# A fused conditional FFN layer: gate and up by tiles of two samples, from gathered rows of weight products

## The chip, the cores and the metric

One core of a Trainium2 chip runs the kernel. Five engines matter: TensorE (PE, matmuls and transposes, with PEld for its weight loads), VectorE (DVE), ScalarE (ACT), GpSimd (POOL) and SyncE (SP, which here only issues DMAs). Each takes its instructions in program order and waits on semaphores. The metric is the device time of one execution in microseconds; a comparison gives the median over rounds on the same chip.

## The reference

There are 32 samples of 64 rows by 1024 numbers, so 2048 rows. Two layers follow one another:

```
x = x + ffn0(cond0(x))    # cond0: a 64x64 matrix per sample; ffn0: W, bias and 8 LoRA terms
x = x + ffn1(cond1(x))    # below
Bx    = einsum('bni,bri->bnr', x,  B[adapter_ids])     # rank 16, own adapter of each sample
cond1 = einsum('bnr,bor->bno', Bx, A[adapter_ids])     # 1024 wide
gate  = cond1 @ Wg.T ;  up = cond1 @ Wu.T              # 2752 hidden units, 4-bit codes
ffn1  = (silu(gate) * up) @ Wd.T                       # codes with a scale per 64
```

The hidden units are 21 chunks of 128 and a tail of 64. Since `cond1` has rank 16 per sample, gate is `Bx @ (A' Wg')`: the kernel multiplies each chunk of the gate and up weights with all 8 adapters' A first, which gives a 128 x 128 product (8 adapters x 16 ranks by 128 hidden units). That is the "weight product" below.

## The kernel before, in words

Single-precision numbers are split into a high and a low part of a rounded 32-bit type (`F32R`), and a product is three matmuls: high x high, high x low, low x high.

**Two phases.** The first phase goes over 16 tiles of 128 rows (two samples each) and computes `x1`, the first layer's output, and from it `Bx` of the second (`adapter_bx`, with a bias). The second phase goes over 96 slots: 6 groups of 3 or 4 chunks (`GROUPS`) times 16 row tiles. A slot is one tile's down matmuls over the group's chunks (`down`), the store of the sum by an accumulating DMA (`accumulate`), and, between them, other work. Slots 80 to 95, the last group, add the result read back from memory instead.

**Decoding.** A unit is the gate part `("g", c)`, the up part `("u", c)` or the down part `("d", c)` of a chunk's weights (`("t", c)`: gate and up of the tail). ScalarE computes the 8 linear functions of the codes (`line`), VectorE folds them by minimum and maximum (`decode`, `combo`) and scales the result. The number of VectorE's steps per slot is planned by `RATE` (`STEPS_B`), and so is the slot in which a unit is turned (`TURN_AT`, `turn_unit`). A turned gate or up unit is multiplied with A by `adapter_ga` in the slot behind it (16 records for 8 full-precision matmuls), near the slot's end. ScalarE copies the product out of PSUM (`evac_ga`, into `ga_f`), and GpSimd splits it (`split_ga`, into `st_hi` and `st_lo`). Units 0 to 11 of gate and up are decoded in the first phase, units 12 to 21 in slots 12 to 72.

**Gate and up.** Before the change `Bx` of a tile is masked by VectorE (`mask_bx`): of the 128 rows (8 adapters x 16) only those of the sample's own adapter are kept, and GpSimd splits it (`split_bx`) into `bx_hi` and `bx_lo`. `gate_up(g, b, k)` makes chunk k of group g for a block b of 512 columns (4 tiles), three matmuls of 512 columns for the gate and three for the up part:

```
for m, ps in enumerate((ps_g, ps_u)):
    for p, (w, v) in enumerate(((st_hi, bx_hi), (st_hi, bx_lo), (st_lo, bx_hi))):
        ins = pe.matmul(ps, w[:, c % ST, m, :], v[:, cols], start=p == 0, stop=p == 2)
```

`gate_ups_at` puts the passes of the next block one by one into the slots of this one. ScalarE takes the SiLU (`silu`), VectorE multiplies (`product`), ScalarE makes the high part (`inter_hi`) and VectorE the low (`inter_lo`) that `down` reads.

**Order.** Every engine's order is written out by hand, slot by slot. GpSimd's in a slot is `split_ga` of the unit turned in the slot before, if there is one, and then `accumulate` of the slot before. In TensorE's slot `gate_up` stands behind the down matmuls of all chunks but the last two, and `adapter_ga` behind all but the last.

## Time and profile before

| what | value |
|---|---|
| median of 3 runs | 1005.73 us (1005.17 to 1006.11) |
| span of the profiled execution, first to last instruction | 1007.3 us |
| TensorE busy | 992.0 us, 98% |
| VectorE busy | 892.6 us, 89% |
| ScalarE busy | 773.8 us, 77% |
| GpSimd busy | 286.6 us, 28% |
| mean granted TensorE clock | 0.994 of full speed |
| DMA | 126.31 MB, mean 125 GB/s |
| share of the chain that ended last | PE 94%, DVE 3%, ACT 1%, DMA 1% |

The profiled execution has no separate time of its own beside its span; the span stands 1.6 us, 0.2%, above the median of the runs. A busy matmul is a record with the length of its whole passage; records overlap, so the cost of one in a stream is the distance between starts. A row of a timeline is start, duration, engine, line and operation (out<-in), the number merged, and in brackets the idle time before it and what ended it.

### The profile page before, as it was taken

What the parts mean: (1) busy time and instruction counts of PE and PEld (TensorE: products, weight loads), DVE (VectorE), ACT (ScalarE), POOL (GpSimd) and SP (SyncE); (2) the same over time, 40 slices, a digit from 0 to 9 for tenths busy, and PEclk for the clock granted to TensorE, in tenths of its full rate; (3) what the DMA queues carried; (4) which work ended last, traced back from release to release, by engine and by line L of the source; (5) the groups of instructions that cost most, each with busy time, mean ns of one, the idle gap of its engine ahead of it and who ended that gap; (6) DMA issues with size and microseconds to landing.
All of it is one profiled execution on the core that took longest, in us unless ns stands there. A gap on an engine that the chain in (4) does not pass through costs nothing.

```text
span 1007.3 us, 15039 instructions
## 1 busy us (share of the span) xinstructions
PE 992.0 (98%) x5314; PEld 849.9 (84%) x5314; DVE 892.6 (89%) x1308; ACT 773.8 (77%) x929; POOL 286.6 (28%) x269
## 2 busy tenths in 40 slices
PE   6999999999999999999999999999999999999998
PEld 5898899889898878888888888888888888888887
DVE  3999999989999979999999999999999999962353
ACT  4788888878878869988888889889888888853220
POOL 4015533633542421132312241113304123321000
PEclk8999999999999999999999999999999999999999
DMA  9846446347334337767475456656465563664766
GB/s 246 220 139 157 101 109 174 87 99 197 86 89 103 71 57 126 144 113 139 68 138 98 95 106 125 108 103 126 89 122 106 104 122 69 124 139 74 195 220 230
DMA packets 73658, 126.31 MB, mean 125 GB/s; under 512 B 7504, under 2 KB 49504, under 8 KB 73584
## 3 DMA queue, kind: packets, MB, share of 16 engines
q0 software_dynamic: 15200, 51.41, 31.8%
q1 hardware_dynamic: 57056, 72.89, 24.4%
q10 hardware_dynamic: 1328, 1.05, 0.3%
q8 instruction: 43, 0.70, 0.3%
q14 instruction: 31, 0.25, 0.1%
HBM read 66.61 MB, written 67.11 MB: 133 GB/s over the span
## 4 chain that ended last, share of the span: by engine, by line
PE 94%; DVE 3%; ACT 1%; DMA 1%; issue 1%; ACTq 0%; DVEq 0%
PE ps_z L1173 23%; PE ps_y L1173 23%; PE ps_z L1017 16%; PE ps_gu L1148 12%; PE ps_gu L1075 4%; PE ps_t L1063 4%; PE ps_t L1075 3%; PE ps_y L1004 3%; PE ps_gu L1035 2%; PE ps_t L1027 1%; DMA la<-in_L_ffn_lora_A 1%; DVE val L789 1%; ACT ring L610 1%; PE ps_z L994 1%; DVE val L791 0%
## 5 line engine op out<-in xcount | busy, mean ns | idle before, releaser
L610 ACT ACTIVATE ring<-codes 128x1024 f32<-128x1024 int32 x455 | 455.3, 1053 | 2.4 <-DVE val L789 1.1
L789 DVE TENSOR_TENSOR val<-val,ring 128x512 f32<-128x512 f32 x520 | 327.8, 689 | 2.5 <-ACT ring L610 2.1
L791 DVE SCALAR_TENSOR_TENSOR val<-ring,val 128x512 f32<-128x512 f32 x390 | 247.8, 690 | 6.0 <-ACT ring L610 5.5
L524 POOL TENSOR_TENSOR st_hi<-ga_f,one 128x128 fp32r<-128x128 f32 x42 | 78.4, 1866 | 227.0 <-ACT ga_f L650 226.9
L582 POOL DMA_DIRECT2D out<-staged x80 | 69.3, 926 | 235.2 <-ACT staged L736 226.3
L722 ACT ACTIVATE inter<-ps_gu 128x512 f32<-128x512 f32 x88 | 52.6, 598 | 92.4 <-PE ps_gu L1148 91.9
L1017 PE MATMUL ps_z<-we_hi,y_hi 128*128 128x512 f32 x256 | 104.7, 409 | 0.2 <-DVE y_lo L850 0.2
L931 DVE TENSOR_TENSOR inter<-ps_gu,inter 128x512 f32<-128x512 f32 x88 | 60.2, 684 | 47.1 <-ACT inter L722 46.2
L1017 PE MATMUL ps_z<-we_hi,y_lo 128*128 128x512 f32 x256 | 100.3, 392 | 0.0
L1017 PE MATMUL ps_z<-we_lo,y_hi 128*128 128x512 f32 x256 | 100.0, 391 | 0.0
L547 POOL TENSOR_TENSOR bx_hi<-bx_f,one 128x128 fp32r<-128x128 f32 x16 | 43.8, 2740 | 142.5 <-DVE bx_f L862 142.5
L1173 PE MATMUL ps_z<-wd_late_hi,in_hi 128*128 128x512 f32 x256 | 81.1, 396 | 0.0
L1173 PE MATMUL ps_y<-wd_late_hi,in_hi 128*128 128x512 f32 x256 | 80.3, 395 | 0.3 <-DVE wd_late_lo L844 0.3
L937 DVE TENSOR_TENSOR in_lo<-inter,in_hi 128x512 fp32r<-128x512 f32 x88 | 61.7, 701 | 17.1 <-ACT in_hi L728 17.0
L1173 PE MATMUL ps_z<-wd_late_lo,in_hi 128*128 128x512 f32 x240 | 74.3, 390 | 0.0
L1173 PE MATMUL ps_z<-wd_late_hi,in_lo 128*128 128x512 f32 x240 | 74.3, 389 | 0.0
L1173 PE MATMUL ps_y<-wd_late_lo,in_hi 128*128 128x512 f32 x240 | 74.0, 390 | 0.0
L1173 PE MATMUL ps_y<-wd_late_hi,in_lo 128*128 128x512 f32 x240 | 74.0, 389 | 0.0
L1148 PE MATMUL ps_gu<-bx_hi,st_hi 128*128 128x512 f32 x176 | 69.3, 394 | 0.7 <-DVE inter L931 0.7
L606 ACT ACTIVATE val<-codes 128x1024 f32<-128x1024 int32 x65 | 68.4, 1053 | 1.8 <-DMA codes<-in_L_ffn_gate_codes 1.8
L1148 PE MATMUL ps_gu<-bx_hi,st_lo 128*128 128x512 f32 x176 | 69.0, 392 | 0.0
L1148 PE MATMUL ps_gu<-bx_lo,st_hi 128*128 128x512 f32 x176 | 69.0, 392 | 0.0
(141 smaller groups left out, 1888.5 us busy)
## 6 DMA issues: line engine op xcount, KB each, us to landing
out<-staged POOLq DMA_DIRECT2D x80, 512.0 KB, 5.6
codes<-in_L_ffn_down_codes SPq DMA_DIRECT2D x21, 512.0 KB, 4.0
xs<-in_x SPq DMA_DIRECT2D x16, 512.0 KB, 4.0
out<-in_L_ffn_bias SPq DMA_DIRECT2D x4, 2048.0 KB, 14.5
out<-xs POOLq DMA_DIRECT2D x16, 512.0 KB, 5.5
ring<-out SPq DMA_DIRECT2D x16, 512.0 KB, 4.3
out<-ring SPq DMA_DIRECT2D x15, 512.0 KB, 2.9
codes<-in_L_ffn_gate_codes SPq DMA_DIRECT2D x12, 512.0 KB, 5.2
```

Of the source, the lines that this page charges most:

```text
L524: pool.tensor_tensor(hi, src, one[:, :].to_broadcast([P, P]), ALU.mult).then_inc(ga_step, 1)
L582: pool.dma_start(out_rows[t * P:(t + 1) * P, :], staged[:, place, :], accum_op=ALU.add).then_inc(acc_out[place], 16)
L606: act.activation(val_of(n), codes[:, n % 2, :], ACT.Relu, bias=offset, scale=slope).then_inc(lines, 1)
L610: act.activation(ring[:, (k - 1) % RING, :], codes[:, n % 2, :], ACT.Identity, bias=offset, scale=slope).then_inc(lines, 1)
L789: ins = dve.tensor_tensor(into, into, line, pick)
L791: ins = dve.scalar_tensor_tensor(out=into, in0=line, scalar=add, in1=into, op0=ALU.add, op1=pick)
L931: dve.tensor_tensor(inter[:, q % 2, :], ps_u[:, :], inter[:, q % 2, :], ALU.mult).then_inc(inter_ready, 1)
L937: dve.tensor_tensor(in_lo[:, b % 2, k, :], inter[:, q % 2, :], in_hi[:, b % 2, k, :].bitcast(F32), ALU.subtract).then_inc(in_lo_ready, 1)
L1017: ins = pe.matmul(ps_z[:, half], y[:, jc, :], w[:, jc, half], start=jc == 0 and p == 0, stop=jc == DC - 1 and p == 2)
L1075: ins = pe.matmul(ga_bank(n), ad_at[:, q, :, :].rearrange("p n r -> p (n r)"), wt[:, m % 2, q, :], start=q == 0, stop=q == DC - 1)
L1148: ins = pe.matmul(ps, w[:, c % ST, m, :], v[:, cols], start=p == 0, stop=p == 2)
L1173: ins = pe.matmul(ps_o[slot % 2][:, h * HALF:(h + 1) * HALF], v[:, b % 2, k, s * P:(s + 1) * P], wd_of(c, w)[:, h * HALF:(h + 1) * HALF], ...
```

## The change

Gate and up are computed per tile of 128 columns (two samples) instead of per block of 512. Instead of three matmuls over 128 masked rows there is one over 96 rows: 2 samples x 16 ranks, three times, the high part twice and the low part once.

- The split products no longer stay on chip. `st_hi` and `st_lo` are 3 places deep (12 before), and SyncE stores each into a table in memory per group (`store_table`).
- For each of the 96 works (group, tile) GpSimd gathers the 96 rows of the two samples' own adapters (high, low, high) by an indirect DMA (`fetch`, into `gath`, 3 places). The row numbers come from `selections` on VectorE, at the kernel's start.
- `bx_p` holds the matching `Bx`: ScalarE adds the bias (`bias_bx`), TensorE puts the own rows of each sample into three places of 32 rows (`place_bx`, three full-precision matmuls), ScalarE writes the high part (`place_hi`) and VectorE the low (`low_bx`). `mask_bx` and `split_bx` are gone.
- `gate_up(w)` is one matmul per chunk for gate and one for up, 6 or 8 per work. It runs two slots ahead (`AHEAD`).
- SiLU, product and the split of `inter` are per work, with widths of 384 or 512.
- Two lines of `BY_GROUP` change, so that gate and up units of groups 4 and 5 are turned some slots earlier than down units.

```diff
-    ST = 12
+    ST = 3
+    INR = 3
+    GS = 3
+    AHEAD = 2
+    FETCH = 4
+    KP = 96
...
-        [("d", 15), ("g", 17), ("u", 17), ("d", 16), ("g", 18), ("u", 18), ("d", 17), ("d", 18)],
-        [("g", 19), ("d", 19), ("u", 19), ("g", 20), ("u", 20), ("d", 20), ("t", TAIL), ("d", TAIL)],
+        [("g", 17), ("u", 17), ("d", 15), ("g", 18), ("u", 18), ("d", 16), ("d", 17), ("d", 18)],
+        [("g", 19), ("u", 19), ("g", 20), ("u", 20), ("t", TAIL), ("d", 19), ("d", 20), ("d", TAIL)],
...
+            def store_table(n):
...
+                sp.wait_ge(ga_split, m + 1)
+                for part, st in enumerate((st_hi, st_lo)):
+                    sp.dma_start(tables[g][part * P:(part + 1) * P, cols],
+                                 st[:, m % ST, :, :].rearrange("p a i -> p (a i)")[:, 0:width].bitcast(F32)
+                                 ).then_inc(table_in[m % ST], 16)
...
+            def fetch(w):
+                g, t, _ = work_of(w)
+                if t == 0:
+                    for k in range(ST):
+                        pool.wait_ge(table_in[k], 16 * 2 * len(range(k, LAST_GU[g] + 1, ST)))
+                if w == 0:
+                    pool.wait_ge(select_step, 8)
+                wait(pool, u_mm, w - GS + 1)
+                width = len(GROUPS[g]) * 2 * P
+                pool.indirect_dma_start(gath[0:KP, w % GS, 0:width].bitcast(F32), None, tables[g][:, :],
+                                        bass.IndirectOffsetOnAxis(ap=row_at[0:KP, t:t + 1], axis=0)
+                                        ).then_inc(gath_in[w % GS], 16)
...
             store_x1(NT - 1)
-            split_bx(NT - 1)
+            for w in range(GS):
+                fetch(w)
...
-            for slot in range(LAST + 1):
+            for slot in range(WORKS):
                 if is_gu(TURN_AT.get(slot - 1)):
                     split_ga(TURN_AT[slot - 1])
-                if slot > 0:
+                if GS <= slot + FETCH - 1 < WORKS:
+                    fetch(slot + FETCH - 1)
+                if 0 < slot <= LAST:
                     accumulate(slot - 1)
...
+            def place_bx(t):
+                pe.wait_ge(select_step, 4)
+                pe.wait_ge(bx_biased, t + 1)
+                wait(pe, bx_split, t)
+                own = place_of[:, PER * t:PER * (t + 1), :].rearrange("p s r -> p (s r)")
+                for part in range(KP // SQ):
+                    ins = pe.matmul(place_bank(t)[part * SQ:(part + 1) * SQ, :], own, bx_f[:, :], start=True, stop=True)
+                ins.then_inc(bx_placed, 1)
...
-            def gate_up(g, b, k):
+            def gate_up(w):
+                g, t, _ = work_of(w)
+                pe.wait_ge(gath_in[w % GS], 16 * (w // GS + 1))
                 if g == 0:
+                    pe.wait_ge(bx_split, t + 1)
+                for m, (ps, free, done) in enumerate(((ps_g, silu_ready, g_mm), (ps_u, inter_ready, u_mm))):
+                    wait(pe, free, w)
+                    for k in range(len(GROUPS[g])):
+                        ins = pe.matmul(ps[:, k * P:(k + 1) * P], gath[0:KP, w % GS, (2 * k + m) * P:(2 * k + m + 1) * P],
+                                        bx_p[0:KP, t * P:(t + 1) * P], start=True, stop=True)
+                    ins.then_inc(done, 1)
```

The order on GpSimd in the second phase, before the change: each pair of splits is followed by accumulates (`out<-staged`), one per slot.

```order
L582 DMA out<-staged 128x1024 x12
L524 TENSOR_TENSOR st_hi<-ga_f,one 128x128
L526 TENSOR_TENSOR st_lo<-ga_f,st_hi 128x128
L582 DMA out<-staged 128x1024 x3
L524 TENSOR_TENSOR st_hi<-ga_f,one 128x128
L526 TENSOR_TENSOR st_lo<-ga_f,st_hi 128x128
```

And of the change, from slot 15 on (L574 and L576 are the two splits, L603 is the gather, L637 the accumulate):

```order
L637 DMA out<-staged 128x1024
L574 TENSOR_TENSOR st_hi<-ga_f,one 128x128
L576 TENSOR_TENSOR st_lo<-ga_f,st_hi 128x128
L603 DMA gath<-table1,row_at 96x1024
L637 DMA out<-staged 128x1024
L603 DMA gath<-table1,row_at 96x1024
L637 DMA out<-staged 128x1024
```

A gather now stands between each split and the accumulate behind it, and one in every other slot as well.

TensorE's order around a product of a unit with A (L1075, `ps_t<-wt,ad_at`), before the change, to the next slot's gate and up pass.

```order
L1075 MATMUL ps_t<-wt,ad_at 128x128 x8
L1173 MATMUL ps_y<-wd_late_hi,in_hi 128x512 x2
L1173 MATMUL ps_y<-wd_late_lo,in_hi 128x512 x2
L1173 MATMUL ps_y<-wd_late_hi,in_lo 128x512 x2
L1173 MATMUL ps_z<-wd_late_hi,in_hi 128x512 x2
L1173 MATMUL ps_z<-wd_late_lo,in_hi 128x512 x2
L1173 MATMUL ps_z<-wd_late_hi,in_lo 128x512 x2
L1173 MATMUL ps_z<-wd_early_hi,in_hi 128x512 x2
L1173 MATMUL ps_z<-wd_early_lo,in_hi 128x512 x2
L1173 MATMUL ps_z<-wd_early_hi,in_lo 128x512 x2
L1148 MATMUL ps_gu<-bx_hi,st_hi 128x512
```

The same in the change (L1174 the product with A, L1271 down, L1246 gate and up), through to the next slot's gate and up pass:

```order
L1174 MATMUL ps_t<-wt,ad_at 128x128 x8
L1271 MATMUL ps_y<-wd_late_hi,in_hi 128x512 x2
L1271 MATMUL ps_y<-wd_late_lo,in_hi 128x512 x2
L1271 MATMUL ps_y<-wd_late_hi,in_lo 128x512 x2
L1271 MATMUL ps_z<-wd_late_hi,in_hi 128x512 x2
L1271 MATMUL ps_z<-wd_late_lo,in_hi 128x512 x2
L1271 MATMUL ps_z<-wd_late_hi,in_lo 128x512 x2
L1271 MATMUL ps_z<-wd_early_hi,in_hi 128x512 x2
L1271 MATMUL ps_z<-wd_early_lo,in_hi 128x512 x2
L1271 MATMUL ps_z<-wd_early_hi,in_lo 128x512 x2
L1246 MATMUL ps_gu<-bx_p,gath 128x128 x8
```

What stands between the product with A and the next gate and up pass is as it was: one chunk of this slot and two of the next. The pass itself is 8 matmuls of 128 columns where 6 of 512 were.

VectorE's first instructions, before the change and then with it (`lb` and `lbq` are made by the operations on `wt`):

```order
L868 TENSOR_SCALAR lw<-lw 128x8
L870 TENSOR_TENSOR wt<-wt,lw 128x1024
L872 COPY lbq<-wt 128x1024
```

```order
L947 TENSOR_SCALAR odd_i<-part_i 128x1
L950 TENSOR_SCALAR ids_rank<-ad_ids 128x32
L952 CAST odd_f<-odd_i 128x1
L954 TENSOR_TENSOR place_of<-ids_rank,less_rank 128x512
L957 SCALAR_TENSOR_TENSOR ids_step<-ids_rank 128x16
L960 TENSOR_SCALAR diag<-odd_f 128x1
L961 COPY diag<-odd_f 128x1
L963 SCALAR_TENSOR_TENSOR ids_own<-ids_step,odd_f,ids_rank 128x16
L966 TENSOR_SCALAR row_at<-ids_own,row_base 96x16
L971 TENSOR_SCALAR lw<-lw 128x8
```

Nine small operations moved ahead of the first one; the second of them needs `ad_ids` from memory.

## Rows read from the trace of the kernel before

**Rows 1.** Busy time by stage; `us, PE busy (x) PEld DVE ACT POOL, PEclk, DMA share, GB/s`

```profile
42.70:350.00 307.30, 307.27 (x1952) 275.14 (x1953) 296.09 (x466) 258.45 (x300) 126.17 (x113) 1.00 0.47 117
...
366.00:893.00 527.00, 526.75 (x2549) 442.89 (x2548) 518.73 (x749) 457.00 (x556) 130.96 (x109) 1.00 0.58 108
...
893.00:1007.30 114.30, 111.02 (x494) 91.70 (x492) 42.86 (x50) 26.01 (x37) 10.52 (x16) 1.00 0.66 184
```

**Rows 2.** Timeline of TensorE, slot 8; start, us, engine, line, operation

```profile
409.30 0.39 PE L1148 MATMUL ps_gu<-bx_hi,st_hi 128*128 128x512 f32 x1
...
410.66 0.61 PE L1173 MATMUL ps_y<-wd_early_hi,in_hi 128*128 128x512 f32 x2
```

**Rows 3.** Timeline of TensorE, full-precision matmuls of 128 weight columns

```profile
201.04 1.95 PE L1075 MATMUL ps_gu<-wt,ad_at 128*128 128x128 f32 x16
...
202.74 0.48 PE L1017 MATMUL ps_z<-we_hi,y_hi 128*128 128x512 f32 x1
...
53.68 1.84 PE L1129 MATMUL ps_gu<-bias_c,ad_bt 128*128 128x1 f32 x16
```

**Rows 4.** Timelines of one turned unit: TensorE, ScalarE, GpSimd, TensorE

```profile
625.02 1.95 PE L1075 MATMUL ps_t<-wt,ad_at 128*128 128x128 f32 x16
...
627.19 0.27 ACT L650 ACTIVATE ga_f<-ps_t 128x128 f32<-128x128 f32 x1
...
627.61 1.83 POOL L524 TENSOR_TENSOR st_hi<-ga_f,one 128x128 fp32r<-128x128 f32 x1 [11.07 <-ACT ga_f L650]
...
629.51 1.32 POOL L526 TENSOR_TENSOR st_lo<-ga_f,st_hi 128x128 fp32r<-128x128 f32 x1
...
630.78 1.75 POOL L582 DMA_DIRECT2D out<-staged  x2
...
630.89 0.39 PE L1148 MATMUL ps_gu<-bx_hi,st_hi 128*128 128x512 f32 x1
```

**Rows 5.** Timelines, GpSimd free and TensorE's next pass: first and last unit

```profile
446.17 1.76 POOL L582 DMA_DIRECT2D out<-staged  x2
...
444.19 0.39 PE L1148 MATMUL ps_gu<-bx_hi,st_hi 128*128 128x512 f32 x1
...
896.73 1.74 POOL L582 DMA_DIRECT2D out<-staged  x2
...
895.98 0.39 PE L1148 MATMUL ps_gu<-bx_hi,st_hi 128*128 128x512 f32 x1
```

**Rows 6.** DMA issues: operation, number, KB each, us to landing

```profile
cond_bd<-in_L_cond_weights POOLq DMA_DIRECT2D x32, 16.0 KB, 2.1
...
ring<-out SPq DMA_DIRECT2D x16, 512.0 KB, 4.3
...
out<-staged POOLq DMA_DIRECT2D x80, 512.0 KB, 5.6
```

**Rows 7.** Timelines of TensorE and GpSimd, hand-over between the phases

```profile
355.85 1.09 PE L1027 MATMUL ps_y<-ident,xs 128*128 128x128 f32 x8 [1.48 <-DVE xs L857]
...
357.66 0.77 PE L1148 MATMUL ps_gu<-bx_hi,st_hi 128*128 128x512 f32 x1 [0.72 <-DVE inter L931]
...
360.36 2.29 PE L1035 MATMUL ps_z<-x1t,ad_bt 128*128 128x128 f32 x16
...
356.42 0.87 POOL L511 DMA_DIRECT2D out<-xs  x1
```

**Rows 8.** Start: GpSimd's timeline, DMA issues, VectorE's timeline

```profile
2.82 0.61 POOL L493 DMA_DIRECT2D ad_ids<-in_itok_B  x1
...
ad_ids<-in_itok_B POOLq DMA_DIRECT2D x1, 16.0 KB, 7.5
...
9.72 0.69 DVE L872 COPY lbq<-wt 128x1024 f32<-128x1024 f32 x1
```

**Rows 9.** Costliest groups and one row of GpSimd's timeline: splits

```profile
L524 POOL TENSOR_TENSOR st_hi<-ga_f,one 128x128 fp32r<-128x128 f32 x42 | 78.4, 1866 | 227.0 <-ACT ga_f L650 226.9
...
203.38 0.40 POOL L524 TENSOR_TENSOR st_hi<-ga_f,one 128x128 fp32r<-128x128 f32 x1 [1.20 <-ACT ga_f L650]
```

323 lines of the change are left out of this document (187 added, 136 removed).

## The prediction, made before the changed kernel ran

> **What bounds the kernel now.** I read the busy time by stage first [rows 1]. The reader is to see two engines full at once: TensorE is busy 307.27 of 307.30 us in the first phase and 526.75 of 527 us in slots 0 to 73, and VectorE is busy 518.73 of the same 527. Only behind 893 us, where decoding is over, has VectorE room (42.86 of 114.30). So a saving on TensorE alone is worth at most 527 - 518.7 = 8.3 us up to slot 73, and its whole size only behind it. ScalarE (457 of 527) and GpSimd (131 of 527) have room by busy time. GpSimd's matters here for its order, not for its load: it stands most of a slot for `ga_f`, then splits it.
>
> **TensorE: what gate and up cost before and after.** A chunk of 512 tokens took 410.66 - 409.30 = 1.36 us for six matmuls, 0.227 us each [rows 2]; 88 of them are 119.7 us. The change puts 64 times 8 and 32 times 6 matmuls of 128 columns there (704). No narrow matmul of the rounded type is in the trace. The nearest rows are full-precision ones, each of which is recorded as two: 16 records take 202.74 - 201.04 = 1.70 us, 0.106 each, and 16 that move one single column take 1.84 us with the tail of the last [rows 3]. Columns moved don't set this; loading 128 weight columns does. The new ones load 128 weight columns each, from 96 rows, so I take 0.11 (the 0.106, and a little for the wide matmul behind). Bounds: a quarter of 0.227, 0.057, below; two records, 0.212, above. With 0.11, 8 cost 0.88 and 6 cost 0.66, in all 77.4 us, 42 less than before. By place: slots 0 to 73 had 71 chunk passes (96.6 us) and get 60 x 0.88 + 14 x 0.66 = 62.0, which is -34.6; slots 74 to 95 had 14 (19.0) and get 4 x 0.88 + 16 x 0.66 = 14.1, which is -5; the rest is in the hand-over between the phases.
>
> The Trainium skill, TensorE: Matmul & The Clock Gate, "Back-to-back issue gap", has a stream of loads and matmuls at 128 columns cost about 81 ns each. The rows have 106 ns, and the rows are used; by the page TensorE would have some 704 x 0.025 = 18 us less to do.
>
> **The new wait, and who stands behind it.** GpSimd's order in a slot s that follows a turned gate or up unit is: split `ga_f` (high, low), then the gather for tile s+3, then the accumulate. TensorE uses tile s+3 in slot s+1, behind the first two of four chunks. In every other slot the gather is issued nearly two slots ahead; in these it is issued only when the split is done. The trace has each step of this already. Adapter product from 625.02; `ga_f` at 627.19; high part at 627.61, low part at 629.51; the next thing GpSimd does starts at 630.78 in the trace; and the gate and up matmul of slot s+1 starts at 630.89 [rows 4]. So there is nothing between GpSimd being free and TensorE's need. There are 19 such units, from the first (GpSimd free 446.17, TensorE there 444.19, 1.98 late) to the last (896.73 against 895.98, 0.75 late) [rows 5]; over all 19 pairs, read in the same way, GpSimd is 0.62 us late in the mean. What comes on top is the gather from issue to landing. Nothing in the trace is a gather; the nearest transfers take 2.1 us for 16 KB, 4.3 for a 512 KB read from memory and 5.6 for a 512 KB accumulate [rows 6]. A gather brings 96 rows of 4 KB, 384 KB, from memory: on the line between 2.1 and 4.3 that is 3.8. Bounds 2.1 and 5.6. So TensorE stands 0.62 + 3.8 = 4.4 us, 19 times: 84 us (52 to 118).
>
> The Trainium skill, DMA: Bandwidth & Descriptors, "Anatomy of one DMA", fits a transfer issued by GpSimd as 2.0 us plus its bytes over 436 GB/s. An estimate by that page is 2.9 us for a gather, and 19 x 3.5 = 67 us of standing instead of 84. That page's line has no descriptor work for rows by index.
>
> Behind the standing matmul on TensorE are the last two chunks of the slot, so nothing can run ahead: the engine takes its instructions in order. VectorE meets the same wait half a slot later, at its product of that tile, and ScalarE at the SiLU. Both are less than a slot ahead, so they stand too and don't get the time back. VectorE's 8.3 us bound no longer matters: 34.6 us of saved matmuls are taken off the 84, and 49.4 stay.
>
> **The clock.** In the hand-over TensorE stood 1.48 and 0.72 us within 3.5 us, and behind it six matmuls took 360.36 - 357.66 = 2.70 us instead of 1.36 (the 1.2 instead of the 2.4 GHz level), and the next sixteen 2.29 instead of 1.95 [rows 7]. That is 1.7 us lost. Some of the 19 stands will do that. The row has it at 2.2 us of standing in all, and other short stands don't show it; I take 8 of 19, 14 us (0 to 32).
>
> **First phase.** `place_bx` adds three full-precision matmuls with 32 weight columns and 128 moved, 15 times here: six records. At 0.106 each that is 0.64 us; at a quarter of 0.227, 0.34 [rows 2, 3]. TensorE is full here, so it all counts: I take 0.5, 7.5 us (5 to 9.6). ScalarE gets the bias and two small scalings per tile, VectorE two small differences for one masking; both have room by [rows 1] (258 and 296 of 307). GpSimd loses `split_bx`, which nothing waited for. The stores of the tables go through SyncE's queue behind loads of codes that it issues early, and are hidden: a table is complete slots before its group's first gather. If that cover failed, the first gather of a group would come a few us late, five times in all.
>
> **Start.** `selections` stands first on VectorE and needs `ad_ids`, issued at 2.82 and landing 7.5 us later, at 10.3, and some 0.5 later still behind four more iotas [rows 8]. Nine small operations (about 2.2 us) and then the scaling of `lb`, which ended with `lbq` at 9.72 + 0.69 = 10.4, bring it to about 15.2. The transposes of it had room for only part of that: I take +2 us (0 to 3).
>
> **Hand-over.** The first gather stands on GpSimd behind the store of the last x1 tile, issued at 356.42 and 0.87 long: it lands at 357.3 + 3.8 = 361.1. The first gate and up matmul waits for it, and so does the transpose of x1 behind it (355.85 before, about 362 now). From there to the first down matmul one gate and up pass less lies in the way, so of 6 us 4 stay (2 to 6) [rows 7].
>
> **Sum.** 1007.3 + 2 + 7.5 + 4 + 84 - 34.6 + 14 - 5 = 1079 us for a profiled span. The span stands 1.6 us above the median of the runs, 1005.73, so 1078.
>
> **Rivals.**
> *A, the forecast.* Its ends: all low, 1007.3 + 7 + 52 - 34.6 - 5 = 1027, all high, 1007.3 + 2 + 9.6 + 6 + 118 + 32 - 34.6 - 5 = 1135; on the scale of the median 1025 to 1134. Chance 0.66.
> *B, the gather's issue is held up as the splits are.* The high part of a split took 1.87 us in the mean and 1.83 in [rows 4], and one of the same size only 0.40 [rows 9]; what differs is what VectorE runs beside it. If writing the gather's descriptors is held up likewise, 1.5 us come on top of each stand, and up to 3: 19 x 2.3 = 44 in the middle, 1122. Against it: two issues of accumulates took 1.75 us in [rows 4], beside the same VectorE work. The Trainium skill, SBUF — State Buffer, has this as a rule (the two engines share a port pair, and descriptors that GpSimd writes wait for it); it would give this rival's time. Chance 0.12.
> *C, a narrow matmul of the rounded type costs two records.* Then 704 x 0.106 = 75 us more, 1152. For it: every 128-column matmul of the trace that isn't a transpose is two records. Against it: the wide ones of this type are one. Chance 0.08.
> *D, faster: the gathers are never waited for.* Then the stands, the clock and the hand-over go, and VectorE is the bound: 1007.3 + 2 + 7.5 - 8.3 - 5 = 1003.5, on the median's scale 1002. The place is GpSimd's order behind a split, the price is the landing. It decides from a mean stand of (34.6 + 5 - 13.5) / 19 = 1.4 us, a landing of 0.8 us behind GpSimd's free moment; the shortest row is 2.1. For it: if VectorE stands more often, the splits end sooner, and the stand shrinks by up to 2 us in part of the slots. Chance 0.14, of it 0.08 faster, 0.03 the same, 0.03 slower.
>
> **How the numbers follow.** A measurement of this kernel can tell about 0.2% from no change. Faster 0.08 and same 0.03 are from D; all the rest, 0.89, is slower. The predicted time is A's, 1078. The range 1020 to 1140 takes A's ends and B; it leaves out D and C, about 0.2.
>
> **What would show it.** Right: in the chain of waits TensorE's first `ps_gu` matmul of a slot waits for the transfer of `gath`, about 19 long times with a mean near 4 us and hardly in the other slots; VectorE's busy share in the slots falls from 98% to about 88%; the granted clock falls below 1.00 there; a gate and up pass of eight takes 0.85 to 0.9 us; a tile of the first phase grows by about 0.5 us. Wrong: `gath` landing before the matmul is reached, a pass of eight at 1.7 us (C), issues of the gather of 3 us (B), or VectorE still at 98% (D).

## The result, and the profile after

The changed kernel takes 1140.92 us in the median of four runs (1139.9 to 1142.35), the kernel before 1005.45 beside it: 1.135 times as long, 95% interval 1.133 to 1.136. The forecast was 1078 us, its range 1020 to 1140. The direction and the place were right, the size was not: 135 us came where 72 were foreseen.

The page's busy times and its chain that ended last, of the kernel after:

```profile
PE 1016.9 (89%) x5586; PEld 870.8 (76%) x5586; DVE 901.1 (79%) x1346; ACT 787.5 (69%) x993; POOL 331.8 (29%) x337
...
PE 67%; DMA 9%; DVE 8%; POOL 6%; ACT 5%; issue 5%; POOLq 0%; DVEq 0%; ACTq 0%
```

Outside the first phase no engine is full any more, and 9% of the chain is transfers. Busy time by stage, the columns as in [rows 1]: first phase, slots 0 to 73, tail:

```profile
43.00:358.50 315.50, 315.50 (x2037) 277.58 (x2037) 297.98 (x476) 267.13 (x343) 56.29 (x85) 1.00 0.50 124
390.00:1030.70 640.70, 544.68 (x2670) 459.44 (x2669) 513.90 (x747) 454.53 (x556) 230.71 (x190) 0.89 0.63 136
1030.70:1140.70 110.00, 106.72 (x536) 89.81 (x534) 49.06 (x64) 29.84 (x49) 23.62 (x25) 1.00 0.82 242
```

Against [rows 1] the middle row has changed. TensorE was busy in all of 527 us; now it is idle for 96 of 640.7, and the clock is 0.89. VectorE's work is what it was (513.90 us; 514.30 in the same slots of the kernel before); only its share has fallen. The waits (us in total, times, longest):

```profile
PE ps_gu L1246 <- DMA gath<-table,row_at: 109.4, 22, 13.4
...
DVE inter L1025 <- PE ps_gu L1246: 92.3, 17, 10.6
...
ACT inter L799 <- PE ps_gu L1246: 172.9, 57, 11.9
```

Of the 22 waits one is the hand-over (13.4), two are below 0.3, and 19, one for each gate or up unit turned in the slots, make 95.6 us, 5.0 in the mean (1.57 to 9.26). VectorE and ScalarE stand behind TensorE in the same places. One of the 19, GpSimd and then TensorE:

```profile
519.43 6.24 POOL L574 TENSOR_TENSOR st_hi<-ga_f,one 128x128 fp32r<-128x128 f32 x1 [10.00 <-ACT ga_f L707]
525.75 0.45 POOL L576 TENSOR_TENSOR st_lo<-ga_f,st_hi 128x128 fp32r<-128x128 f32 x1
526.35 0.96 POOL L603 DMA_INDIRECT gath<-table,row_at  x1
...
530.49 1.97 PE L1246 MATMUL ps_gu<-bx_p,gath 96*128 96x128 f32 x8 [7.50 <-DMA gath<-table,row_at]
532.26 1.16 PE L1271 MATMUL ps_z<-wd_late_hi,in_hi 128*128 128x512 f32 x2
...
537.49 1.13 PE L1162 MATMUL ps_t<-ident,val 128*128 128x128 f32 x8
...
541.23 1.01 PE L1246 MATMUL ps_gu<-bx_p,gath 96*128 96x128 f32 x8
542.07 0.68 PE L1271 MATMUL ps_y<-wd_late_hi,in_hi 128*128 128x512 f32 x2
```

GpSimd stands 10 us for `ga_f`, its high part takes 6.24 us instead of the 0.40 of [rows 9], and only then is the gather issued. TensorE, idle for 7.5 us, then runs at the 1.2 GHz level: the pass of eight takes 532.26 - 530.49 = 1.77 us, and twelve wide matmuls 537.49 - 532.26 = 5.23 us, 0.436 each. From 541.23 the same pass takes 0.84 us, 0.105 a matmul: one record each, as forecast.

The gather (duration of the issue in ns, min/median/max, and us to landing), and two plain transfers of the page (number, KB each, us to landing):

```profile
L603 POOL DMA_INDIRECT gath<-table,row_at x96: 914/969/4074, 367.1 to 1115.1; - x96
...
DMA to landing us min/median/max: 3.5/6.4/9.5
```

```profile
out<-staged POOLq DMA_DIRECT2D x80, 512.0 KB, 6.5
...
ring<-out SPq DMA_DIRECT2D x16, 512.0 KB, 5.7
```

Over all 96 gathers the landing is 6.4 us in the median, above the bound of 5.6, and the plain transfers have slowed too, from 5.6 and 4.3 [rows 6]. For the 19 gathers that TensorE stands for it goes on again sooner, 4.58 us behind their issue in the mean (4.11 to 6.47; here 530.49 - 526.35 = 4.14). They are issued 0.45 us in the mean behind the moment at which TensorE is there (from 2.5 us before it to 4.3 behind it), which makes 5.03 us a stand. The median of all mixes two kinds. In the slots, these 19 gathers alone are issued with no other transfer of GpSimd under way, and land after 4.5 us in the mean; the other 54 are issued while an accumulate is, and land after 7.2. The hand-over, TensorE and GpSimd:

```profile
360.37 0.42 PE L1134 MATMUL ps_gu<-bx_f,place_of 128*32 128x128 f32 x6
360.72 1.09 PE L1162 MATMUL ps_t<-ident,val 128*128 128x128 f32 x8
375.22 1.51 PE L1246 MATMUL ps_gu<-bx_p,gath 96*128 96x128 f32 x6 [13.40 <-DMA gath<-table,row_at]
...
361.61 1.13 POOL L574 TENSOR_TENSOR st_hi<-ga_f,one 128x128 fp32r<-128x128 f32 x1 [11.77 <-ACT ga_f L707]
...
365.92 0.86 POOL L562 DMA_DIRECT2D out<-xs  x1 [1.78 <-DMA table<-st_hi]
367.09 1.03 POOL L603 DMA_INDIRECT gath<-table,row_at  x1 [0.31 <-issue]
```

Two things stand ahead of the first gather: the last split of the first phase, which waits for the last `ga_f` and ends at 364.14, and the store of the last x1 tile. By the code the store waits for VectorE's last `xs`, which ends at 365.06 (the bracket names another transfer), so here the store decides. The gather lands 7.9 us behind its issue, with that store under way ahead of it.

**The sum, forecast and measured** (spans; slots from copy of `staged` to copy of `staged`):

| term | forecast | measured |
|---|---|---|
| start | +2 | +0.3 (first phase from 43.0, was 42.7; see e16) |
| first phase | +7.5 | +8.0 |
| hand-over | +4 | +10.8 |
| 19 stands | +84 | +95.6 |
| clock in the slots | +14 | about +50 (e3) |
| gate and up, slots 0 to 73 | -34.6 | about -27, as the rest of +118.2 |
| tail | -5 | -3.9 |
| sum | +72 | +133.4 |

The last row is measured between the two profiled executions; the medians lie 135.5 us apart.

### The profile page after: what moved, and what is told of

It reads as the page before. It is cut to its first block, busy times and chain, and to the rows that moved or that the text cites. A ratio compares the mean times of both kernels' runs of the same rounds, so it can differ in the third digit from the quotient of the medians.

```text
span 1140.7 us, 16184 instructions
## 1 busy us (share of the span) xinstructions
PE 1016.9 (89%) x5586; PEld 870.8 (76%) x5586; DVE 901.1 (79%) x1346; ACT 787.5 (69%) x993; POOL 331.8 (29%) x337
## 4 chain that ended last, share of the span: by engine, by line
PE 67%; DMA 9%; DVE 8%; POOL 6%; ACT 5%; issue 5%; POOLq 0%; DVEq 0%; ACTq 0%
PE ps_y L1271 15%; PE ps_z L1271 14%; PE ps_z L1107 14%; DMA gath<-table,row_at 8%; PE ps_gu L1246 7%; POOL st_hi L574 4%; PE ps_gu L1174 3%; PE ps_t L1162 3%; ACT ring L667 3%; DVE val L863 3%; PE ps_t L1174 2%; PE ps_y L1094 2%; PE ps_gu L1125 2%; DVE val L865 1%; PE ps_t L1117 1%
## 5 line engine op out<-in xcount | busy, mean ns | idle before, releaser
L1246 PE MATMUL ps_gu<-bx_p,gath 96*128 96x128 f32 x704 | 106.9, 299 | 109.4 <-DMA gath<-table,row_at 109.4
L1246 PEld LDWEIGHTS ps_gu<-bx_p,gath 96*128 96x128 f32 x704 | 105.5, 218 | 124.4 <-DMA gath<-table,row_at 104.9
L574 POOL TENSOR_TENSOR st_hi<-ga_f,one 128x128 fp32r<-128x128 f32 x42 | 65.1, 1550 | 375.4 <-ACT ga_f L707 355.5
L799 ACT ACTIVATE inter<-ps_gu 128x512 f32<-128x512 f32 (+1 forms) x96 | 53.9, 561 | 173.6 <-PE ps_gu L1246 172.9
L1025 DVE TENSOR_TENSOR inter<-ps_gu,inter 128x512 f32<-128x512 f32 (+1 forms) x96 | 61.8, 644 | 130.8 <-PE ps_gu L1246 92.3
L637 POOL DMA_DIRECT2D out<-staged x80 | 76.7, 959 | 219.5 <-ACT staged L812 219.5
L603 POOL DMA_INDIRECT gath<-table,row_at x96 | 111.8, 1164 | 63.7 <-PE ps_gu L1246 40.9
L1032 DVE TENSOR_TENSOR in_lo<-inter,in_hi 128x512 fp32r<-128x512 f32 (+1 forms) x96 | 63.0, 656 | 36.3 <-ACT in_hi L805 36.0
L1271 PE MATMUL ps_y<-wd_late_hi,in_hi 128*128 128x512 f32 x256 | 88.7, 430 | 0.0
L1271 PE MATMUL ps_z<-wd_late_hi,in_hi 128*128 128x512 f32 x256 | 86.8, 419 | 0.0
L1271 PE MATMUL ps_y<-wd_late_lo,in_hi 128*128 128x512 f32 x240 | 79.3, 413 | 0.0
L1271 PE MATMUL ps_z<-wd_late_lo,in_hi 128*128 128x512 f32 x240 | 78.0, 406 | 0.0
L1271 PE MATMUL ps_y<-wd_late_hi,in_lo 128*128 128x512 f32 x240 | 77.5, 405 | 0.0
L1271 PE MATMUL ps_z<-wd_late_hi,in_lo 128*128 128x512 f32 x240 | 77.1, 402 | 0.0
L805 ACT ACTIVATE in_hi<-inter 128x512 fp32r<-128x512 f32 (+1 forms) x96 | 56.8, 592 | 20.7 <-DVE inter L1025 20.4
## 6 DMA issues: line engine op xcount, KB each, us to landing
out<-in_L_ffn_bias SPq DMA_DIRECT2D x4, 2048.0 KB, 14.3
```

The lines of the kernel that those rows point to most:

```text
L574: pool.tensor_tensor(hi, src, one[:, :].to_broadcast([P, P]), ALU.mult).then_inc(ga_step, 1)
L603: pool.indirect_dma_start(gath[0:KP, w % GS, 0:width].bitcast(F32), None, tables[g][:, :], bass.IndirectOffsetOnAxis(ap=row_at[0:KP, t:t + ...
L637: pool.dma_start(out_rows[t * P:(t + 1) * P, :], staged[:, place, :], accum_op=ALU.add).then_inc(acc_out[place], 16)
L1025: dve.tensor_tensor(inter[:, w % 2, 0:width], ps_u[:, 0:width], inter[:, w % 2, 0:width], ALU.mult).then_inc(inter_ready, 1)
L1032: dve.tensor_tensor(lo, inter[:, w % 2, 0:width], hi.bitcast(F32), ALU.subtract).then_inc(in_lo_ready, 1)
L1246: ins = pe.matmul(ps[:, k * P:(k + 1) * P], gath[0:KP, w % GS, (2 * k + m) * P:(2 * k + m + 1) * P], bx_p[0:KP, t * P:(t + 1) * P], start= ...
```

## The experiments

Where a version's time is given with an interval, it is its ratio to the kernel before, run beside it. "Slots" is the time of slots 0 to 73: 522.5 us before, 640.7 after.

**The order of the units alone** (`b6_group_order_alone`), put into the kernel before:

```
-        [("d", 15), ("g", 17), ("u", 17), ("d", 16), ("g", 18), ("u", 18), ("d", 17), ("d", 18)],
+        [("g", 17), ("u", 17), ("d", 15), ("g", 18), ("u", 18), ("d", 16), ("d", 17), ("d", 18)],
(and the next group likewise)
```

> The kernel before with only the order of the units in the last two groups with decoding taken from the changed kernel (gate and up units of a group ahead of its down units). Theory (this part of the change costs and brings nothing): 1005.5 us within 0.2%. Rival (a unit of down that is turned later delays the first down matmul of its group): 1 to 4 us slower.

Measured: 1005.66 us, 0.9996 (0.9986 to 1.0006). This part costs nothing.

**The gather ahead of the split** (`e1_gather_first`), in the changed kernel:

```
             for slot in range(WORKS):
+                if GS <= slot + FETCH - 1 < WORKS:
+                    fetch(slot + FETCH - 1)
                 if is_gu(TURN_AT.get(slot - 1)):
                     split_ga(TURN_AT[slot - 1])
-                if GS <= slot + FETCH - 1 < WORKS:
-                    fetch(slot + FETCH - 1)
```

> The changed kernel with two statements of GpSimd's slot exchanged: the gather for tile s+3 is issued before the split of the turned unit, not behind it. Nothing else differs. Theory (the order on GpSimd makes the stands, and the stands make the half clock): the 19 long waits of gate and up for a transfer of gath go, with them 95.6 us of standing and some 55 to 60 us of matmuls at the 1.2 GHz level. VectorE is then the bound in slots 0 to 73, at 514 to 522 us instead of 641; the hand-over (about 11 us) and the first phase (about 8 us) stay. So 1005.5 + 19 - 4 - (0 to 8) = 1012 to 1020 us, I say 1016, granted clock 1.00 in the slots. Rival 1 (the gather itself is too slow, 6.4 us in the median and more in a busy stretch, whatever the order): waits of several us stay in at least half of the slots, above 1060 us. Rival 2 (the issue of the gather, 1 us, now delays the split, so the high and low parts, the store of the table and the copy of the next ga_f come later and something new waits): 1025 to 1045 us.

Measured: 1058.25 us, 1.0515 (1.0483 to 1.0548), slots 556.4. So 83 us go with two exchanged statements, but not the 125 expected: 54.2 us of standing are left in 16 waits, 40.9 of it outside the hand-over. My theory was right in kind and incomplete; rival 1's stands are there, though 11 of the 15 are below 3 us, and the time is just below its 1060.

**And the first gathers ahead of the last x1 store** (`e2_gather_first_early_start`): `for w in range(GS): fetch(w)` is moved above `store_x1(NT - 1)`.

> As the kernel with the gather ahead of the split, and besides the first three gathers are issued before the store of the last x1 tile instead of behind it. The tables of the first group are complete long before. Theory (the hand-over's 13.4 us of standing is this issue order: the store waits for VectorE's last sum, then the gather takes 6.4 us): the stand goes, 9 to 12 us less than the kernel before it, 1003 to 1009 us. Rival (the store has to be there before anything else can start, since the accumulates or the last tile's bx_p are late anyway): within 3 us of the kernel with the gather ahead of the split.

Measured: 1047.71 us, 1.040 (1.0365 to 1.0435). The first wait falls from 13.3 to 6.8 us, and 10.5 us go by the medians, as expected (7.8 by the profiled spans, 1056.5 and 1048.7). The time itself is not the 1003 to 1009 expected, since e1 came out higher. The hand-over in e2:

```profile
364.08 1.03 POOL L603 DMA_INDIRECT gath<-table,row_at  x1 [0.17 <-issue]
...
368.41 1.51 PE L1246 MATMUL ps_gu<-bx_p,gath 96*128 96x128 f32 x6 [6.81 <-DMA gath<-table,row_at]
```

The gather is issued 2.8 us earlier than in e1, and with no store ahead of it it lands after 4.1 us instead of 7.8. So more than half of the gain is the landing. It is a stand that e1 left which tells what is still wrong; here in the trace of e2, GpSimd and then TensorE:

```profile
451.42 4.82 POOL L574 TENSOR_TENSOR st_hi<-ga_f,one 128x128 fp32r<-128x128 f32 x1 [5.76 <-ACT ga_f L707]
456.31 0.46 POOL L576 TENSOR_TENSOR st_lo<-ga_f,st_hi 128x128 fp32r<-128x128 f32 x1
456.89 0.94 POOL L637 DMA_DIRECT2D out<-staged  x1
458.13 1.90 POOL L603 DMA_INDIRECT gath<-table,row_at  x1 [0.30 <-issue]
...
464.77 1.97 PE L1246 MATMUL ps_gu<-bx_p,gath 96*128 96x128 f32 x8 [6.04 <-DMA gath<-table,row_at]
```

The gather of this slot was ahead of the split, but the next one stands behind it, and an accumulate of 512 KB goes before it too. TensorE has it 6.6 us after its issue. The late gather has moved by one tile.

**The stands filled with work** (`e3_fill_the_stands`), the changed kernel in its own order:

```
             def gate_up(w):
                 g, t, _ = work_of(w)
+                if w in late:
+                    wait(pe, silu_ready, w)
+                    for _ in range(FILL[late.index(w)]):
+                        pe.matmul(ps_g[:, 0:HALF], bx_p[0:KP, 0:P], bx_p[0:KP, 0:HALF], start=True, stop=True)
```

> The changed kernel in its own order, and TensorE is given matmuls without use for the time that it stood: ahead of the gate and up of the tile whose gather is late, 7 to 41 wide matmuls into ps_g, as many as 0.227 us fit into the stand that the trace showed at that place (423 in all, 96 us). They change no result, since the real ones overwrite them. Theory (the half clock behind each stand costs as much again as a good half of the standing): the clock stays at 1.00 in the slots, the standing is replaced one for one, and 40 to 60 us go, 1080 to 1100 us. Rival (the loss behind a stand is not the clock but ScalarE and VectorE, which have to refill their lead of less than a slot): no gain, 1130 to 1145 us. Less than 20 us of gain with a clock of 1.00 would speak for the rival too.

Measured: 1102.62 us, 1.0966 (1.0946 to 1.0986), slots 599.8. The slots' row, and the same stretch for the useless matmuls alone (TensorE, its weight loads):

```profile
389.00:988.80 599.80, 593.30 (x3093) 501.55 (x3092) 513.87 (x747) 451.91 (x557) 234.81 (x190) 1.00 0.67 146
...
389.00:988.80 599.80, 99.46 (x423) 79.52 (x423) 1.00 0.67 146
```

Nothing is earlier for anyone, TensorE only does useless matmuls where it stood, and the slots are 41 us shorter at a granted clock of 1.00. The rival, no gain, is out; by the medians 38 us go, just short of the 40 to 60 expected. The 41 us are less than what the half clock cost: the useless matmuls and 6.2 us of standing that is left make some 6 to 10 us more than the 95.6 that they replace. TensorE's own work tells the cost more directly. Without the useless matmuls it takes 593.3 - 99.5 = 494 us here, and 544.7 in the changed kernel: about 50 us are the clock. Both do the same matmuls. The kernel before needed 522.5 for its own, so the change saves TensorE about 28 us in the slots. Added up from start to start, gate and up take 60.7 us here against 95.2 before, the 34.6 that were forecast; but the 1662 wide matmuls of `down` take 387.4 against 380.7, which the forecast had left as they were.

**One slot more of lead, two ways** (`e4_one_slot_earlier`, `e5_one_slot_earlier_old_order`): `FETCH = 5` instead of 4, and the fourth gather issued behind the first three; e4 on top of e2, e5 in the changed kernel's own order.

> The kernel with the gather ahead of the split and the first gathers early, and now each gather is issued one slot earlier still: FETCH is 5 instead of 4. No buffer is added: the buffer of tile w is free when gate and up of tile w-3 is done, which is in slot w-5. In the two kernels with the gather ahead of the split a stand of about 6 us is left in 16 to 19 slots, one slot later than in the changed kernel: there the split took 4.82 us for its high part instead of 0.4 and the next gather stood behind it and landed 6.6 us later. Theory (what is left is the gather behind a held-up split, and one slot of lead covers it): no stand is left, granted clock 1.00, and VectorE is the bound in slots 0 to 73, 514 to 522 us instead of 562: 1047.7 - 44 = 1004 us (998 to 1010). Rival (with no stands at all the gathers' traffic or GpSimd's own time decides, slots stay above 530 us): 1015 to 1035.

> The changed kernel in its own order (split ahead of the gather, the first gathers behind the store of the last x1 tile), with FETCH 5 instead of 4 alone. The gather behind the split of a unit turned in slot s is now for tile s+5 instead of s+4. Theory (it is the lead that counts, whichever way it is got): the same stands as in the kernel with the gather ahead of the split, since there too the gather behind a split is for tile s+5: 1058 us, 1050 to 1066. Rival (the order itself counts, since the issue of a gather ahead of the split delays it or the split's hold-up depends on it): over 10 us from 1058.

Measured: e4 1015.3 us, 1.0068 (1.0038 to 1.0097), slots 520.7; e5 1033.91, 1.0279 (1.0254 to 1.0304), slots 523.5. Three executions of e5 took 1025 to 1036 us; a fourth took 2496, which nothing here explains, and the ratio leaves it out. The time of e4 is at the low end of the rival's, its slots are where the theory had them. Both have the gather behind a split for tile s+5, as e1 has, and e5 still comes out some 25 us below e1: I expected the same time. In e5 the gather behind the split goes ahead of the accumulate, in e1 it goes behind it, and the medians of landing are 6.5 and 7.2 us. So lead counts most, and the order of split, gather and accumulate on GpSimd counts too.

In e4 nearly all stands are gone. One long one is left, 10.6 us of TensorE:

```profile
864.36 14.33 POOL L581 TENSOR_TENSOR st_hi<-ga_f,one 128x64 fp32r<-128x64 f32 x4 [4.98 <-ACT ga_f L709]
...
890.02 1.97 PE L1248 MATMUL ps_gu<-bx_p,gath 96*128 96x128 f32 x8 [10.61 <-DMA gath<-table,row_at]
```

Four pieces of 128x64 take 14.3 us on GpSimd, the same four 3.4 us in e2. The runs of e4 lie between 1006 and 1018 us.

**Who bounds the slots now** (`e6_one_slot_earlier_half_lo` on e4, `b7_before_half_lo` on the kernel before): the subtraction `inter_lo` is done for half of its columns.

```
+                if not (w < INR or NT <= w < NT + INR):
+                    width //= 2
                 dve.tensor_tensor(lo, inter[:, w % 2, 0:width], hi.bitcast(F32), ALU.subtract).then_inc(in_lo_ready, 1)
```

> The kernel with FETCH 5, the gather ahead of the split and the first gathers early, with the low part of the product (inter_lo on VectorE) computed for one half of its columns only, behind the first tiles of the first two groups: it leaves out half of that subtraction, and the old low part stays in the other half. VectorE has some 74 x 0.27 = 20 us less to do in slots 0 to 73. Theory (VectorE alone bounds the slots once no gather is late, and the 35 us that TensorE saves there can't be had): 12 to 22 us faster than the same kernel with the whole subtraction, 984 to 992. Rival (something else bounds it): within 4 us of the kernel with the whole subtraction.

> The kernel before with the same half of inter_lo left out (behind the first tiles of the first two groups; the old low part stays in the other half). Theory (there TensorE is full in the slots, 526.75 of 527 us, so less work on VectorE brings nothing): 1002 to 1006 us. Rival (VectorE was as much the bound as TensorE): 990 to 998.

Measured: e6 991.12 us, 0.985 (0.9834 to 0.9867), 24 us below e4; b7 1005.61, 0.9998 (0.9988 to 1.0008). The same edit brings nothing where TensorE is full and much where the gathers are nearly in time. VectorE is then the bound, as [rows 1] said. Not all of the 24 us are its work: VectorE is busy 17 us less in the slots (492.6 against 510.0), and the stand of 10.6 us in e4 is one of 2.1 here.

**The high part off GpSimd, in the changed kernel's order** (`e7_high_part_on_scalar`): ScalarE writes `st_hi` behind its copy to `ga_f`, and GpSimd's first operation is gone.

```
-                act.activation(ga_f[:, m % 2, :], ga_bank(n), ACT.Copy).then_inc(ga_evac, 1)
+                act.activation(ga_f[:, m % 2, :], ga_bank(n), ACT.Copy)
+                if m >= ST:
+                    act.wait_ge(table_in[m % ST], 16 * 2 * (m // ST))
+                act.activation(st_hi[:, m % ST, 0, :], ga_bank(n), ACT.Copy).then_inc(ga_evac, 1)
```

> The changed kernel in its own order, but the high part of each split is written by ScalarE, straight from the bank behind its copy to ga_f; GpSimd keeps the low part alone. In the changed kernel GpSimd's high parts take 1.55 us in the mean and from 0.4 to several us. Theory (that is GpSimd held up by VectorE, and each stand contains it): the high part then costs some 0.25 us on ScalarE, each of the 19 stands is about 1.3 us shorter, clock as before: 1141 - 25 = 1116 us (1106 to 1124). Rival (the hold-up moves to the low part, whichever operation of GpSimd comes next): 1132 to 1142.

Measured: 1115.92 us, 1.1079 (1.1054 to 1.1105): 25.0 us less, the number that was computed, but not in the way that it was. The 19 stands are 0.84 us shorter each (4.19 in the mean, was 5.03), not 1.3, which makes 16 us; the other 10 are TensorE's work in the slots, 534.8 us where it was 544.6, so fewer of its matmuls ran at the half clock. In front of these 19 gathers the high parts took 2.54 us in the mean, more than the 1.55 over all, and the low parts behind them 0.81; now the low parts alone take 2.53. So two thirds of the hold-up moved to the next operation, as the rival had it, and that the sum fits is luck.

**A plain transfer in the gather's place** (`e8_plain_gather`):

```
-                pool.indirect_dma_start(gath[0:KP, w % GS, 0:width].bitcast(F32), None, tables[g][:, :],
-                                        bass.IndirectOffsetOnAxis(ap=row_at[0:KP, t:t + 1], axis=0)
+                pool.dma_start(gath[0:KP, w % GS, 0:width].bitcast(F32), tables[g][0:KP, :]
```

> The changed kernel with the gather by index replaced by a plain transfer of the same size in the same place: rows 0 to 95 of the table, 384 KB, into the same buffer. It leaves out the selection of the own adapters' rows, so the gated values are those of other rows. Theory 1 (the gather by index is what makes 6.4 us out of the 3.8 that I took from plain transfers): it lands 4.3 to 4.6 us behind its issue and 19 x 2 = 38 us go, 1095 to 1110 us. Theory 2 (it is what else is on the way, the accumulate ahead of it and the loads): it lands as late as before, 1130 to 1142 us.

Measured: 1133.68 us, 1.1246 (1.1199 to 1.1293). Its rows of DMA issues:

```profile
gath<-table POOLq DMA_DIRECT2D x64, 384.0 KB, 7.2
```

A plain transfer of the same bytes lands no sooner: 6.7 us in the median over all 96 (6.4 by index), 4.5 in the mean with no other transfer of GpSimd under way (4.5) and 7.9 behind an accumulate (7.2). Theory 2: the landing is no matter of the index. It goes with what GpSimd has under way; how the time splits between the queue and the memory is not shown. The 7 us that e8 gains are beyond the intervals; the issue of a plain transfer is shorter on GpSimd, 0.83 us in the mean against 1.22 (380 to 900 us), and whether that is the reason is not shown.

**The high part on ScalarE with FETCH 5** (`e9_split_off_the_gathers_way`): e4, the edit of e7, and `accumulate(slot - 1)` ahead of the split.

> The kernel with FETCH 5, the gather ahead of the split and the first gathers early, and besides: the high part of each split on ScalarE, and GpSimd issues the accumulate of a slot before the split instead of behind it. There the split of the last unit took 14.3 us for its four high pieces and 3.7 for its four low ones while VectorE worked without a pause, one gather was late by 13.4 us, and the runs lay between 1006 and 1018 us. Theory (GpSimd's held-up splits are the last thing that makes a gather late): no stand left, 1015 - 16 = 999 us (996 to 1003), and the runs within 3 us of each other. Rival (the low pieces are now held up as long): 1008 to 1016 us.

Measured: 1010.55 us, 1.0045 (1.0028 to 1.0061): the rival. The trace has the same hold-up one operation further, the four low pieces, and beside them VectorE without a pause:

```profile
864.66 14.25 POOL L575 TENSOR_TENSOR st_lo<-ga_f,st_hi 128x64 fp32r<-128x64 f32 x4 [5.26 <-ACT st_hi L704]
...
864.66 6.75 POOL L575 TENSOR_TENSOR st_lo<-ga_f,st_hi 128x64 fp32r<-128x64 f32 x1 [5.26 <-ACT st_hi L704]
...
864.60 3.68 DVE L862 TENSOR_TENSOR val<-val,ring 128x512 f32<-128x512 f32 x6
868.21 0.67 DVE L1031 TENSOR_TENSOR in_lo<-inter,in_hi 128x512 fp32r<-128x512 f32 x1
...
871.15 0.67 DVE L1024 TENSOR_TENSOR inter<-ps_gu,inter 128x512 f32<-128x512 f32 x1
```

The pieces end 14 us later in a stretch in which VectorE's rows follow each other without an idle time. Two of the four take nearly all of it, 6.75 and 6.97 us; the other two take 0.32 each. The Trainium skill, SBUF — State Buffer, "Who interferes with whom", has a VectorE operation with two inputs in SBUF and a GpSimd operation that reads SBUF exclude each other, for the whole instruction of whichever is first. The trace agrees that GpSimd is the one that waits, but it waits through ten and more instructions of VectorE, mostly of 0.6 us, not through one. Both long pieces end 0.26 us behind the start of VectorE's product (L1024), one of whose inputs is `ps_gu` in PSUM and not in SBUF; it comes once a slot.

**No arithmetic on GpSimd in the slots** (`e11_no_split_on_gpsimd`, the changed kernel in its own order and lead; `e12_low_part_on_vector`, on e9): the low part of unit s is one operation of VectorE in slot s+2, `low_ga(TURN_AT[slot - 2])`, and GpSimd's `split_ga` in the slots is gone.

> The changed kernel in its own order and with FETCH 4, but in the slots no split is on GpSimd: ScalarE writes the high part behind its copy to ga_f, VectorE the low part one slot later (some 0.25 us, 19 times). GpSimd then only issues gathers and accumulates. Theory (a gather is late only because it stands behind a split that waits for ga_f; its 6.4 us are hidden as soon as it is issued at its slot's start): no stand in slots 0 to 73, VectorE is the bound there, 505 to 520 us instead of 641, and the hand-over stays: 390 + 512 + 110 = 1012 us (1008 to 1020). Rival (a landing of 6.4 us, up to 9.5, is too long for the lead that FETCH 4 gives even without a split ahead): stands stay, over 1030 us.

> The kernel with FETCH 5 and the high parts on ScalarE, with the low parts of the slots on VectorE instead of on GpSimd. Theory (the last stand, behind four pieces that took 14.3 us on GpSimd, is what is left; VectorE pays 19 x 0.25 = 5 us): the stand of some 6 us and its clock go, and 5 us come, 1010.6 - 8 + 5 = 1007 us (1003 to 1010). Rival (the stand cost nothing, since VectorE is the bound through it): 1013 to 1016.

Measured: e11 1011.53 us, 1.0054 (1.0035 to 1.0074), slots 510.5; e12 1007.57, 1.0020 (1.0009 to 1.0031), slots 510.5. In the order and with the lead of the changed kernel, and with its gathers, 129 of the 135 us are gone. The waits and the gather's rows of e11:

```profile
PE ps_gu L1260 <- DMA gath<-table,row_at: 11.7, 2, 11.5
...
L590 POOL DMA_INDIRECT gath<-table,row_at x96: 915/1640/5217, 368.2 to 983.1; - x96
...
DMA to landing us min/median/max: 3.4/6.6/10.4
```

The gathers land as late as ever, 6.6 us, and nobody waits but the hand-over (and once for 0.15 us). That settles what makes a stand: the order behind `ga_f`, not a landing of this length. Both times are where the theories had them, and VectorE is busy 509.3 of the 510.5 us.

**Some turns on TensorE** (`e10_some_turns_on_tensor` on e9; `e13_low_part_on_vector_some_turns_on_tensor` on e12): 8 of the 19 units are turned by TensorE and copied by ScalarE.

```
+    PE_TURNED = [('g', 13), ('g', 14), ('g', 15), ('g', 16), ('u', 17), ('u', 18), ('u', 19), ('u', 20)]
     def on_dve(n):
-        return UNITS[n][0] != "d" and n >= PHASE_A_UNITS
+        return UNITS[n][0] != "d" and n >= PHASE_A_UNITS and UNITS[n] not in PE_TURNED
```

> As the kernel with the high parts on ScalarE and FETCH 5, and 8 of the 19 gate and up units of the slots are turned by TensorE and ScalarE (as the down units are) instead of by VectorE. A turn takes 2.22 us on VectorE; on TensorE 16 records, about 1.75 us, and a copy of 1.05 us on ScalarE. Theory (VectorE bounds the slots, TensorE has some 20 us of room there): VectorE gives back 8 x 2.2 = 18 us and TensorE has room for 14: 10 to 17 us faster than the same kernel without it, 984 to 990 us. Rival (TensorE is then full, or the unit's later turn delays its product and table): within 4 us of it, or slower.

> The kernel with 8 of the 19 turns on TensorE, and the low parts of the slots on VectorE instead of on GpSimd. There 8.9 us of standing were left. Theory (the stands and their clock were on the path, and VectorE has given back more than the 5 us it gets): 1000.9 - 11 + 5 = 995 us (992 to 999). Rival (VectorE is still the bound through them): 1003 to 1006.

Measured: e10 1000.9 us, 0.9949 (0.9932 to 0.9965), slots 506.1; e13 1000.0, 0.9938 (0.9923 to 0.9953), slots 505.0. e10 gives 9.7 us against e9, a little under the 10 to 17 expected, and is not near the 984 to 990 that were built on e9's theory. TensorE is full again in both, 504 of 506 and of 505 us, so the slots can't get shorter this way. e13 lies between its theory and its rival: in e10 only one stand of 1.25 us outside the hand-over was left, so there was next to nothing to take.

**The hand-over and the start** (`e14_first_gathers_before_last_split` on e12, `e15_same_with_some_turns_on_tensor` on e13, `e16_same_and_selections_later` on e15). GpSimd and TensorE in e12:

```profile
365.24 1.08 POOL L571 TENSOR_TENSOR st_lo<-ga_f,st_hi 128x128 fp32r<-128x128 f32 x1 [12.49 <-ACT st_hi L698]
366.48 1.82 POOL L590 DMA_INDIRECT gath<-table,row_at  x1 [0.17 <-issue]
...
373.30 1.51 PE L1262 MATMUL ps_gu<-bx_p,gath 96*128 96x128 f32 x6 [7.82 <-DMA gath<-table,row_at]
```

The same fault as in the slots: the first gather behind a split that waits for `ga_f`.

```
             for t in range(NT):
+                if t == NT - 1:
+                    for w in range(GS):
+                        fetch(w)
                 if t > 0:
                     store_x1(t - 1)
```

> The kernel with FETCH 5, high parts on ScalarE and the low parts of the slots on VectorE, all 19 turns on VectorE, and the first three gathers issued a tile earlier on GpSimd, ahead of the last tile's splits. Theory (the 7.8 us of standing in the hand-over are these splits, and the half clock behind them costs some 3 to 4 us): 1007.6 - 11 = 997 us (994 to 1000), so the narrow gate and up by gathered rows is then faster than the kernel before, with nothing else moved. Rival (VectorE has its own backlog at the hand-over and bounds it): 1004 to 1008.

> The same with 8 of the 19 turns on TensorE. Theory: 1000.0 - 11 = 989 us (986 to 993). Rival (something else bounds the hand-over): 996 to 1000.

> The same again, and VectorE computes the selections behind the scaling of lb and its copy lbq instead of ahead of them, so that TensorE's transposes of lbq don't wait for the ids of the adapters. Theory (the start costs nothing by the time the first phase runs, since TensorE's keep_warm matmuls and the weights' loads cover it): within 1 us of the kernel without it. Rival (the 2 us that I priced it at): 2 to 4 us faster.

Measured: e14 1001.8 us, 0.9959 (0.9946 to 0.9973); e15 995.28, 0.9897 (0.9882 to 0.9912); e16 991.44, 0.986 (0.9845 to 0.9875). In e14 and e15 no wait for a gather is left at all. e14 gives 5.8 us by the medians and 9.0 by the profiled spans (1008.6 and 999.6), between theory and rival. e15 gives 4.7 us against e13, just faster than its rival's 996 and not the 11 of its theory. e16 gives 3.8 us where I expected none: the rival. TensorE's row at the transposes of `lbq` and at the first matmul of the first phase, in e15 and then in e16:

```profile
14.89 1.97 PE L1208 MATMUL ps_t<-ident,lbq 128*128 128x128 f32 x8 [7.41 <-DVE lbq L992]
...
43.63 0.47 PE L1126 MATMUL ps_z<-we_hi,y_hi 128*128 128x512 f32 x1 [0.22 <-DVE y_lo L924]
```

```profile
10.47 1.97 PE L1208 MATMUL ps_t<-ident,lbq 128*128 128x128 f32 x8 [1.45 <-DVE lbq L991]
...
39.92 0.47 PE L1126 MATMUL ps_z<-we_hi,y_hi 128*128 128x512 f32 x1 [0.17 <-DVE y_lo L924]
```

The 4.4 us at `lbq` arrive as 3.7 at the first phase. Why then was the start of the changed kernel only 0.3 us later than before? Two rows of the profile of the kernel before, and the same two of b6, which has the same start:

```profile
13.84 1.06 ACT L670 ACTIVATE bx_hi<-la 128x1024 fp32r<-128x1024 f32 x1 [9.93 <-DMA la<-in_L_ffn_lora_A]
...
42.73 0.47 PE L1017 MATMUL ps_z<-we_hi,y_hi 128*128 128x512 f32 x1 [0.22 <-DVE y_lo L850]
```

```profile
10.73 1.06 ACT L670 ACTIVATE bx_hi<-la 128x1024 fp32r<-128x1024 f32 x1 [6.83 <-DMA la<-in_L_ffn_lora_A]
...
40.06 0.47 PE L1017 MATMUL ps_z<-we_hi,y_hi 128*128 128x512 f32 x1 [0.17 <-DVE y_lo L850]
```

In the profiled execution of the kernel before, the load of `la` landed at 13.8 us, later than in any other profile here (10.3 to 13.2), and the first phase began 2.6 us later than in b6. In b6 and b7 it begins at 40.1 and 40.2, so in the changed kernel, at 43.0, it is 2.9 us later.

## Why the prediction was wrong in size

**What bounds the kernel** was right: TensorE and VectorE, with VectorE just behind. e6 and b7 show it from both sides.

**The cost of the narrow matmuls** was right: 0.105 us each, 0.84 for eight and 0.64 for six, against 0.11 taken. Rival C is out. The saving of 34.6 us is there on gate and up, but the down matmuls give 6.7 of it back (e3), so TensorE has some 28 us less to do in the slots. Even once the gathers are in time only 12 us of it come (522.5 to 510.5 in e11 and e12), the 8.3 us that VectorE's idle time allowed and a little more.

**The new wait** was right in place, number and mechanism: 19, at the second slot behind each turned unit, behind the split on GpSimd. The mean was 0.45 + 4.58 = 5.03 us against 0.62 + 3.8 = 4.4 (95.6 against 84), so the mis-sized piece is the landing, "on the line between 2.1 and 4.3 that is 3.8": 4.58 where it is stood for, within the bounds. e8 shows that its excess is no matter of the index. The landing is this short where GpSimd has stood for `ga_f` and has nothing else under way; while an accumulate is under way it is 7.2 in the mean.

**The clock** is the step that failed: "I take 8 of 19, 14 us (0 to 32)". 18 of the 19 did it, the shortest of 1.57 us among them; only behind one of 2.23 us were the wide matmuls at full speed throughout. Each of the 18 cost about 50 / 18 = 2.8 us, not 1.7, since the low level held on for 3 to 7.5 us of work. So the term was about 50 us (e3: 41 of them go when the stands are filled), above the end of my range, and its excess of 36 us is more than half of the 61 by which the sum was off. I had read it from a row with 2.2 us of standing in which the engine was back soon [rows 7], and took the rarity there for a rarity here, where the stands are twice as long. The trace before had a nearer case that I had not used, at the start:

```profile
18.93 0.80 PE L994 MATMUL ps_z<-bx_hi 128*128 128x512 f32 x1 [4.96 <-DVE bx_lo L877]
```

Behind these 5 us of standing the next nine wide matmuls take 22.93 - 18.93 = 4.00 us instead of 2.04.

**The hand-over**, "+4 (2 to 6)", was 10.8. I had put the first gather behind the store of x1, and that was where it stood. But the landing was 7.9 us and not 3.8, with the store under way ahead of it (4.1 in e2), and I had no half clock in this term: the matmuls behind the stand took about 4.5 us more than at the full level, against 1.7 before. The split, which I had not counted, ended 0.9 us before the store could start; it is the next thing in the way once the store is moved (e12 and e14). e2 and e14 took 10.5 and 5.8 us by moving the gathers ahead of the one and the other.

**First phase and tail**: 8.0 and -3.9 against 7.5 and -5. The six records of `place_bx` take 360.72 - 360.37 = 0.35 us, the low bound, 4.9 us in all. The other 3.1 us are in matmuls that were there before, in the same number: the wide ones take 182.0 us instead of 180.5, the transposes 22.1 instead of 21.2, the products with A 40.6 instead of 39.9. So 7.5 was near for a reason that I had not seen.

**The start** came as +0.3 against +2, but not since it was free: e16 shows that the selections cost 3.7 us there, and against b6 and b7 the start is 2.9 us later, near the forecast and within its 0 to 3. The profiled execution of the kernel before was itself late there, and that hid the price. By the same 2.6 us its span stands above the median of the runs, where those of b6 and b7 stand 2.5 below theirs; with its 2.6 us added, the 133.4 of the sum are 136.0, beside 135.5 by the medians.

**Rival B** (the gather's issue is held up) is out for the changed kernel: median 0.97 us, and none of the 19 that TensorE stood for is over 1.25, though 12 of the 60 issues between 380 and 900 us are over 1.3. **Rival D** (never waited for) is not what the change does. e11 shows that it is what the same gathers do when nothing waits ahead of them, and its time, 1002, would have been 9.5 us too low, about the size of the hand-over, which it leaves out.

## What to carry to other kernels

When a transfer is issued by an engine that also computes, ask what that engine waits for just ahead of the issue: one instruction that waits for late data turns every hidden landing behind it into a stand, and the price of the transfer itself hardly matters. Stands on TensorE are to be priced with the clock: here 1 us of standing cost another 0.5 us. And where a change frees one engine while another is full by 98%, move some work over to the freed one in the same step: of some 28 us, 12 came alone, and eight turns moved to TensorE brought 6.5 to 9.7 more.

## What the hardware did that was not expected

GpSimd's issue of a gather is held up as its arithmetic is, once VectorE works without pauses: mean 1.22 us in the changed kernel (380 to 900 us), 1.66 in e9, 2.56 in e12, single ones up to 5.2 in e9 and e12. It cost nothing there, since the gathers had lead. The issue of a plain transfer in the same place is not held up: none over 1.2 us in e8.

A GpSimd operation that takes 0.4 us can take 6.2, and four of a quarter microsecond 14.3, beside a full VectorE. What lets it through can be read in e9: of the 14 low parts in the slots that take over 1 us, each ends 0.26 to 0.41 us behind the start of VectorE's product, which reads PSUM, or of its scaling (L892), and none between the 0.6 us operations that stand back to back around them. Why the scaling lets it through is not shown. Such a piece on GpSimd has no price that can be read from one row; its spread, 1006 to 1018 us in e4, is the mark of it.

The best version, e16, takes 991.44 us, 1.4% less than the kernel before: the changed kernel's gate and up, no arithmetic on GpSimd in the slots, the first gathers a tile earlier, eight turns on TensorE, and the selections behind `lbq`.
